# Zeroing the masked exponentials on GpSimd in place of a mask product on TensorE

## The chip, the cores and the metric

The kernel runs on one core of one Trainium2 chip. The metric is the device time of one launch in microseconds (us), lower is better; of the kernel before there are three runs. All engine names are those of the profile: PE is TensorE (PEld its weight loads), ACT ScalarE, DVE VectorE, POOL GpSimd, SP the engine that issues most DMAs.

## The reference, cut to what matters

32 sequences of 256 rows and 256 features attend to 77 context rows in 16 heads of 16, with a causal mask that lets row t see context rows 0 to t. A gated feed-forward with a shared part and a routed part of 8 experts follows.

```python
scores = jnp.einsum('bhqd,bhkd->bhqk', qh, kh) / jnp.sqrt(jnp.asarray(dh, q.dtype))
pad = mask[:, None, None, :]
causal = jnp.triu(jnp.ones((Sq, Sk), dtype=jnp.int32), k=1)[None, None]
merged = jnp.where(causal == 1, causal, pad)
scores = jnp.where(merged == 1, NEG_INF, scores)
attn = jax.nn.softmax(scores, axis=-1)
out = jnp.einsum('bhqk,bhkd->bhqd', attn, vh)
...
x = x + jnp.tanh(g_xattn[0]) * _L0_xattn_ref(_layernorm(x, axis=-1), ctx_1024, ctx_1024, L0_xattn_W, L0_xattn_b, mask_BxS2_if0)
x = x + jnp.tanh(g_ffn[0]) * _L0_ffn_ref(_layernorm(x, axis=-1), L0_ffn_w_in, L0_ffn_w_out, L0_ffn_w1, L0_ffn_w2, L0_ffn_wg, L0_ffn_we, L0_ffn_gb, L0_ffn_eb)
```

With 77 context rows the mask touches only the first 77 of the 256 query rows, a corner of 77 by 77 in every head.

## The kernel before

The kernel has two phases. Phase one runs attention, the shared feed-forward (`ffn`) and the routing for all sequences; phase two runs the experts tile by tile. The change lies in phase one.

**One list sets the order.** `phase_one` (L60) writes a list of stages `(name, b, k)`, and each engine walks through this same list and issues its own part of each stage, in order. So an engine that waits in one stage holds up all later stages on that engine. A pass i of the outer loop has 12 slots. Sequence b passes through them as a pipeline: its layer norm in pass b, its row maxima (`max`) in pass b+1, its scores, exponentials, values and the transposes `att` in pass b+2, its projection (`proj`), second norm and `x2T` in pass b+3. Below, "pass of sequence b" is the pass with the scores of b. After every second slot (1, 3, 5, 7, 9, 11) two pieces of the shared feed-forward are put into the list, 24 pieces for each pair of sequences. A piece below 16 is three matmuls of 512 columns (L712), a later one six of 256 (L729).

**Scores and values.** A step `scores` k handles four heads: four products of 256 columns (L620) into a pair of PSUM banks. Before them come two products of 154 columns (L615) that write the causal mask `cauT` (0 or -3e38) through the bf16 identity `identb` into the corners of the banks; the scores are added onto it. ACT turns the pair into exponentials `Pt` (L891), and each such step counts up the semaphore `P`. A step `values` k multiplies eight heads of `Pt` with `Vau` (L632) and waits for `P` of scores 2k+1, so for two exponentials.

**What GpSimd does.** In the order of the list: `bias` (L1449) adds the projection's bias to `x1`, once the DMA of `load_x1` (L500, issued by SP in slot 11 of the pass before) has landed; `keys` (L1424) spreads the keys, twice in each pass; `low` (L1375) makes the low part `gl` of the feed-forward's hidden values, at every pair of pieces with part 1, after ACT wrote the high part `gh` (L853), which ACT does behind the tanh (L932) of the same pair; `root` (L1382, L1384) takes the inverse square roots of the norms; `first` (L1442) adds the causal mask for the maxima; and in a routing round eight indirect DMAs scatter records (L1473), one at each piece of the list. Rounds (`ROUTES`, L43) come about every fourth pass.

**Places of the stages in a pass.** Before: scores in slots 1, 3, 5 and 7, values 0 in slot 5, values 1 in slot 8, `att` in slot 11. In slot 3 of each pass POOL has `keys` and a `low`; in the pass of an even sequence it also has a `low` in slot 7.

Of the kernel before, what the change touches and what calls it, by code (L numbers as in the profile page):

```python
# [7 lines left out]
BF = mybir.dt.bfloat16  # L8
I32 = mybir.dt.int32
ALU = mybir.AluOpType  # L10
# [3 lines left out]
P = 128  # L14
NB, S, D, K = 32, 256, 256, 77
# [6 lines left out]
NEG = -1e30  # L22
NEGP = -3e38
NEGB = -2.5e38
# [14 lines left out]
    "idb m8 ks0 va_zero va_one ones rec pre_zero pre wgh0 lb0 tgh brow pbias crow kcol ks1".split())}  # L39
GCON = {n: i + 7 for i, n in enumerate("ident caus cauT upb kint fold foldb".split())}  # L40

# [18 lines left out]
def phase_one():  # L60
# [31 lines left out]
    for i in range(NB + 3):  # L92
        slots = [[] for _ in range(12)]

        def put(b, stages):
            if 0 <= b < NB:
                for slot, name, k in stages:
                    slots[slot].append((name, b, k))

        if i % 2 == 1:  # L100
            put(i - 4, ((2, "logits", 0), (5, "logitsT", 0)))
            if i < NB + 1:
                put(i - 4, ((6, "store_x2", 0),))
        put(i - 2, ((1, "scores", 0), (3, "scores", 1), (5, "scores", 2), (5, "values", 0), (7, "scores", 3), (8, "values", 1),
                    (5 if i < 6 else 11, "load_x1", 0), (11, "att", 0)))
# [91 lines left out]
def build(nc, A, out):  # L197
    ctx = ExitStack()
    with ctx:
# [9 lines left out]

# [1 line left out]

# [3 lines left out]
        s = {n: ctx.enter_context(nc.semaphore("s_" + n)) for n in names.split()}  # L215
# [48 lines left out]
        sb = sbs(ctx)  # L264
        regr = sb("regr", [P, REG], R)
        ident = sb("ident", [P, P])
        Pt = sb("Pt", [P, H, S])
# [23 lines left out]
        sb = sbs(ph1)  # L291
# [12 lines left out]
        Xs = carve(KR, [2, 4, 2, S])  # L304
# [8 lines left out]
        identb = sb("identb", [P, P], BF)  # L313
        own8 = sb("own8", [P, 8])
        caus = sb("caus", [P, K], BF)
        cauT = sb("cauT", [K, K], BF)
        mhalf = sb("mhalf", [P, 2])
# [3 lines left out]
        fold = sb("fold", [20, 10])  # L321
# [5 lines left out]
        first = sb("first", [P, 2, K], BF)  # L327
# [4 lines left out]
        mr = sb("mr", [P, 2, 2])  # L332
# [11 lines left out]
        gl = sb("gl", [P, 4, 512], R)  # L344
        LGg = sb("LGg", [P, 16, 2])
        LGe = sb("LGe", [P, 16, 8])
        upb = sb("upb", [P, P], BF)
# [14 lines left out]
        kint = sb("kint", [P, 1], I32)  # L362
# [34 lines left out]
        ix = stage[:, 3232:3238].bitcast(I32).rearrange("p (j k) -> p j k", j=3)  # L397
# [5 lines left out]
        sb = sbs(ph2)  # L403
# [157 lines left out]
        def tensor(e):  # L561
            for stage_, b, k in order:
                h = b % 2
# [12 lines left out]
                elif stage_ == "max":  # L576
                    if k == 0:
                        e.wait_ge(s["xTh"], b + 1)
                    t, c = k // 2, k % 2
# [21 lines left out]
                elif stage_ == "scores":  # L601
                    if k == 0:
                        if b == 0:
                            e.wait_ge(s["ks1"], 1)
                            e.wait_ge(s["gcon"], GCON["cauT"])
                        if b == G:
                            e.wait_ge(s["ks1"], 2)
                        e.wait_ge(s[f"kd{ks}"], 96 * (b // G // 2 + 1))
                        e.wait_ge(s[f"xs{h}"], 48 * (b // 2 + 1))
                        e.wait_ge(s[f"mt{h}"], 16 * (b // 2 + 1))  # L610
# [3 lines left out]
                    for n in range(2):  # L614
                        e.matmul(pair[0:K, n, :].rearrange("k (j t) -> k j t", j=2)[:, :, 0:K], identb[0:K, 0:K],  # L615
                                 cauT[:, :].unsqueeze(1).broadcast_to([K, 2, K]), start=True, stop=False, skip_group_check=True)
                    for n in range(2):
                        p, bk = 2 * k + n, pair[:, n, :]
                        for j in range(2):
                            m = e.matmul(bk[0:K, j * S:(j + 1) * S], Kst[:, ks, j, p % 4, 2 * g + p // 4, :],  # L620
                                         Xs[:, h, p % 4, p // 4, :], start=False, stop=j == 1, skip_group_check=True)
                    m.then_inc(s["sc"], 1)
                elif stage_ == "values":
# [3 lines left out]
                    e.wait_ge(sem, v)  # L627
                    e.wait_ge(s["P"], 4 * b + 2 * k + 2)
                    for q in range(2):
# [22 lines left out]
                elif stage_ == "proj":  # L652
# [6 lines left out]
                    for t in range(2):  # L659
                        n = 0  # L660
# [698 lines left out]
        def gpsimd(e):  # L1359
# [17 lines left out]
            def root(n, b):  # L1377

                e.wait_ge(s[f"mom{n}"], 2 * b + 2)
                if b >= 1:  # L1380
# [6 lines left out]
            e.memset(caus[:, :], 0.0).then_inc(s["gcon"], 1)  # L1387
            e.memset(cauT[:, :], 0.0).then_inc(s["gcon"], 1)
            e.memset(upb[:, :], 1.0).then_inc(s["gcon"], 1)
            e.memset(mhalf[:, :], -0.5).then_inc(s["gcon"], 1)  # L1390
            e.memset(fold[:, :], 0.0).then_inc(s["gcon"], 1)
            e.wait_ge(s["gcon"], 6)
            e.affine_select(out=ident[:, :], in_=ident[:, :], compare_op=ALU.not_equal, fill=1.0, base=0,
                            pattern=[[-1, P]], channel_multiplier=1).then_inc(s["gcon"], 1)
            e.affine_select(out=caus[:, :], in_=caus[:, :], compare_op=ALU.is_ge, fill=NEG, base=0,
                            pattern=[[-1, K]], channel_multiplier=1).then_inc(s["gcon"], 1)
            e.affine_select(out=cauT[:, :], in_=cauT[:, :], compare_op=ALU.is_ge, fill=NEGP, base=0,
                            pattern=[[1, K]], channel_multiplier=-1).then_inc(s["gcon"], 1)
            e.affine_select(out=upb[:, :], in_=upb[:, :], compare_op=ALU.is_ge, fill=0.0, base=-1,
# [8 lines left out]
            for stage_, b, k in order:  # L1408
# [8 lines left out]
                elif stage_ == "keys":  # L1417
                    if k == 0:
# [3 lines left out]
                        if b >= 2:  # L1422
                            e.wait_ge(s["mm"], 4 * (b - 1))
                    e.tensor_tensor(Kbd[:, b % G, k, :, :], khi[:, b % G * 2 + k, :].bitcast(F).unsqueeze(1).broadcast_to([P, 8, K]),  # L1424
                                    own8[:, :].unsqueeze(2).broadcast_to([P, 8, K]), ALU.mult).then_inc(s["kbd"], 1)
                elif stage_ == "moments":
                    root(0, b)
# [127 lines left out]
```

## Time and profile before

| what | value |
|---|---|
| device time, median of three runs | 1164.55 us (1162.37 to 1165.7) |
| span of the profiled execution, first to last instruction | 1154.6 us |
| phase one in it | about 0 to 680 us |
| PE busy | 1105.4 us (96%) |
| DVE busy | 820.0 us (71%) |
| POOL busy | 519.1 us (45%) |
| ACT busy | 470.4 us (41%) |
| granted PE clock, mean over the span | 0.987 |

The device time of the profiled execution is not listed apart; its span is 9.95 us under the median of the runs, which lies around the instructions. Busy shares are means over stages with different limits. Because PE's matmuls overlap, its cost is read from the distance between starts, not from durations. In the timelines a row merges equal instructions that follow each other, with the first start, the length and the count; in square brackets stands the idle time of the engine before it and what ended that.

### The profile page before, as it was taken

How to read it: one execution, taken by the hardware profiler on the slowest of the kernel's cores; microseconds unless marked ns; L12 is line 12 of the kernel's file. 1: busy time of each engine (PE TensorE's matmuls, PEld its weight loads, DVE VectorE, ACT ScalarE, POOL GpSimd, SP SyncE). 2: the span in 40 equal slices, each digit the busy share in tenths (PEclk: the TensorE clock that was granted, in tenths of full speed). 3: DMA queues.
4: the chain of work that ended last, by engine and by line, in shares of the span. 5: the costliest groups of instructions: out<-in, count | busy, mean ns of one | idle time of the engine just before them, and what ended most of it. 6: DMA issues, size and time to landing. Idle time of an engine off the chain costs nothing.

```text
span 1154.6 us, 22482 instructions
## 1 busy us (share of the span) xinstructions
PE 1105.4 (96%) x7475; PEld 917.9 (80%) x7475; DVE 820.0 (71%) x1778; ACT 470.4 (41%) x722; POOL 519.1 (45%) x647
## 2 busy tenths in 40 slices
PE   5789999999999999999999899999999899999997
PEld 3557888787887788788788677788888788888886
DVE  7757686786786876876877576557544588888886
ACT  4565556545555555555654432223221111111111
POOL 5334447347356346456454523100000666666564
PEclk9989999999999999999999999999999899999999
DMA  8984647656665765764755311587662554555451
GB/s 158 242 191 80 145 98 128 132 118 107 136 125 93 148 131 115 123 141 102 118 117 109 70 46 38 199 263 236 209 211 93 162 160 150 164 162 157 147 177 65
DMA packets 106163, 160.65 MB, mean 139 GB/s; under 512 B 28828, under 2 KB 70718, under 8 KB 106048
## 3 DMA queue, kind: packets, MB, share of 16 engines
q1 hardware_dynamic: 94276, 121.18, 46.0%
q0 software_dynamic: 11776, 38.03, 10.6%
q8 instruction: 65, 1.06, 0.4%
q14 instruction: 46, 0.38, 0.1%
HBM read 75.24 MB, written 52.10 MB: 110 GB/s over the span
## 4 chain that ended last, share of the span: by engine, by line
PE 72%; DVE 10%; issue 8%; POOL 6%; ACT 2%; DMA 1%; POOLq 0%; ACTq 0%; DVEq 0%
PE ps L767 15%; PE ps L814 12%; PE ps L712 8%; PE ps L816 6%; PE ps L729 6%; PE ps L632 4%; PE ps L620 3%; PE ps L663 3%; PE ps L799 3%; POOL tab_dram L1473 2%; PE ps L586 2%; PE ps L590 2%; PE ps L615 1%; PE ps L697 1%; PE ps L686 1%
## 5 line engine op out<-in xcount | busy, mean ns | idle before, releaser
L814 PE MATMUL ps<-regr,gh 128*128 x600 | 221.5, 407 | 0.1
L891 ACT ACTIVATE Pt<-ps,pbias 77x1024 f32<-77x1024 f32 x128 | 141.4, 1105 | 107.4 <-PE ps L620 106.2
L816 PE MATMUL ps<-regr,gl 128*128 x600 | 170.0, 283 | 0.0
L814 PEld LDWEIGHTS ps<-regr,gh 128*128 128x128 f32 x600 | 113.8, 190 | 23.6 <-issue 0.5
L981 ACT ACTIVATE gh<-ps 128x512 fp32r<-128x512 f32 x75 | 44.8, 599 | 204.5 <-PE ps L799 204.5
L1192 DVE TENSOR_REDUCE mneg<-ps 128x8 f32<-128x616 f32 x128 | 100.5, 792 | 19.7 <-PE ps L590 19.6
L816 PEld LDWEIGHTS ps<-regr,gl 128*128 128x128 f32 x600 | 114.2, 190 | 0.0
L712 PE MATMUL ps<-x2h,winh 128*128 128x512 f32 x256 | 110.6, 432 | 0.5 <-DVE OHR L1096 0.5
L1375 POOL TENSOR_TENSOR gl<-gf,gh 128x512 fp32r<-128x512 f32 x64 | 82.5, 1290 | 50.4 <-ACT gh L853 50.1
L712 PE MATMUL ps<-x2h,winl 128*128 128x512 f32 x256 | 101.5, 396 | 0.0
L712 PE MATMUL ps<-x2l,winh 128*128 128x512 f32 x256 | 101.2, 395 | 0.0
L1449 POOL TENSOR_TENSOR x<-x,regf 128x512 f32<-128x512 f32 x32 | 41.1, 1284 | 130.4 <-DMA x<-in_x 130.4
L1361 POOL DMA_INDIRECT yt<-y_dram,Pt x73 | 75.5, 1035 | 53.2 <-PE ps L816 42.7
L1499 POOL DMA_INDIRECT out<-ot,Pt x75 | 77.6, 1035 | 41.3 <-issue 27.9
L1287 DVE SCALAR_TENSOR_TENSOR Pt<-Pt,ps 128x512 f32<-128x512 f32 x64 | 44.0, 688 | 69.0 <-ACT Pt L975 67.8
L975 ACT ACTIVATE Pt<-ps 128x512 f32<-128x512 f32 x64 | 38.3, 598 | 129.8 <-PE ps L767 129.8
L620 PE MATMUL ps<-regr 100*77 100x256 f32 x512 | 87.9, 295 | 0.0
L767 PE MATMUL ps<-regr,x2h 128*128 128x512 f32 x256 | 82.4, 396 | 0.0
L1424 POOL TENSOR_TENSOR regr<-regr,own 128x616 fp32r<-128x616 f32 x64 | 78.4, 1226 | 5.7 <-ACT regr L862 5.4
L1473 POOL DMA_INDIRECT tab_dram<-rec,slot x64 | 64.7, 1011 | 26.7 <-issue 13.3
L1320 DVE SCALAR_TENSOR_TENSOR ot<-ps,Pt,ot 128x256 f32<-128x256 f32 x150 | 72.6, 484 | 5.4
L632 PE MATMUL ps<-Pt,regf 77*32 77x256 f32 x1024 | 69.5, 389 | 6.1 <-ACT Pt L891 6.1
(201 smaller groups left out, 2681.7 us busy)
## 6 DMA issues: line engine op xcount, KB each, us to landing
regr<-regr SPq DMA_DIRECT2D x96, 256.0 KB, 5.9
y_dram<-Pt SPq DMA_DIRECT2D x64, 256.0 KB, 2.2
regf<-in_x SPq DMA_DIRECT2D x32, 256.0 KB, 2.9
x<-in_x SPq DMA_DIRECT2D x32, 256.0 KB, 7.2
y_dram<-res SPq DMA_DIRECT2D x32, 256.0 KB, 2.2
regr<-regr SPq DMA_DIRECT2D x96, 77.0 KB, 6.9
x_dram<-x2h SPq DMA_DIRECT2D x14, 512.0 KB, 3.0
x_dram<-x2l SPq DMA_DIRECT2D x14, 512.0 KB, 3.8
```

The costliest lines, as they stand in the source:

```text
L620: m = e.matmul(bk[0:K, j * S:(j + 1) * S], Kst[:, ks, j, p % 4, 2 * g + p // 4, :], Xs[:, h, p % 4, p // 4, :], start=False, stop=j == 1, ...
L632: m = e.matmul(bk[32 * j:32 * j + 32, q * S:(q + 1) * S], Vau[:, ks, g, n, :], Pt[0:K, n, :], start=True, stop=True)
L712: m = e.matmul(bk[:, :], w[:, cc, off:off + P], x[:, b % 2, cc, :], start=cc == 0 and n == 0, stop=cc == 1 and n == 2)
L767: i = e.matmul(bk[:, :], x[:, cc, k * P:(k + 1) * P], w[:, cc, half * 512:half * 512 + 512], start=n == 0, stop=n == 5)
L814: e.matmul(o, gh2[:, k % 3, fc, :], w2v[:, bass.ds(val, 1), fc, :, :].rearrange("p o h d -> p (o h) d"), start=fc == 0, stop=False, skip_g ...
L816: m = e.matmul(o[:, 0, :], gl2[:, k % 3, fc, :], w2v[:, bass.ds(val, 1), fc, 0, :].rearrange("p o d -> p (o d)"), start=False, stop=fc == ...
L891: e.activation(Pt[0:K, 4 * k:4 * k + 4, :].rearrange("k (n j) t -> k n (j t)", n=2), bank_of["sc", b, k][0:K, :, :], ACT.Exp, bias=pbias[: ...
L1192: e.tensor_reduce(mneg[:, h, t, :].rearrange("p (j q c) -> p c j q", j=2, c=2)[:, c], bank_of["mm", b, k][:, :, 0:4 * K].rearrange("p q (f ...
L1375: e.tensor_tensor(gl[:, fc, :], gf[:, n % 2, :], gh[:, fc, :].bitcast(F), ALU.subtract).then_inc(s["gl"], 1)
L1424: e.tensor_tensor(Kbd[:, b % G, k, :, :], khi[:, b % G * 2 + k, :].bitcast(F).unsqueeze(1).broadcast_to([P, 8, K]), own8[:, :].unsqueeze(2 ...
L1473: e.indirect_dma_start(tab, bass.IndirectOffsetOnAxis(ap=slot[:, j:j + 1], axis=0), rec[:, j, :], None, bounds_check=NC * NT - 1, oob_is_e ...
L1499: e.indirect_dma_start(out.rearrange("b s d -> (b s) d"), bass.IndirectOffsetOnAxis(ap=rt[:, k, 0:1].bitcast(I32), axis=0), ot[:, k % 8, : ...
```

## The change

The mask product L615 and its table `cauT` go. The scores now start the banks themselves (start=True). A new stage `causal` k, on GpSimd alone, waits for the exponentials of scores 2k+1 (`P`) and writes zero over the masked corner of eight heads in `Pt`, in place, 77 partitions by 8 by 77 elements, with one `affine_select`; it counts up the new semaphore `cz`. The step `values` k now waits for `cz` in place of `P`. In the list `causal` 0 stands in slot 4 and `causal` 1 in slot 8, values 0 moves from slot 5 to slot 6, and values 1 from slot 8 to slot 9.

```diff
-        put(i - 2, ((1, "scores", 0), (3, "scores", 1), (5, "scores", 2), (5, "values", 0), (7, "scores", 3), (8, "values", 1),
+        put(i - 2, ((1, "scores", 0), (3, "scores", 1), (4, "causal", 0), (5, "scores", 2), (6, "values", 0), (7, "scores", 3),
+                    (8, "causal", 1), (9, "values", 1),
                     (5 if i < 6 else 11, "load_x1", 0), (11, "att", 0)))
...
                     for n in range(2):
-                        e.matmul(pair[0:K, n, :].rearrange("k (j t) -> k j t", j=2)[:, :, 0:K], identb[0:K, 0:K],
-                                 cauT[:, :].unsqueeze(1).broadcast_to([K, 2, K]), start=True, stop=False, skip_group_check=True)
-                    for n in range(2):
                         p, bk = 2 * k + n, pair[:, n, :]
                         for j in range(2):
                             m = e.matmul(bk[0:K, j * S:(j + 1) * S], Kst[:, ks, j, p % 4, 2 * g + p // 4, :],
-                                         Xs[:, h, p % 4, p // 4, :], start=False, stop=j == 1, skip_group_check=True)
+                                         Xs[:, h, p % 4, p // 4, :], start=True, stop=True)
...
                     e.wait_ge(sem, v)
-                    e.wait_ge(s["P"], 4 * b + 2 * k + 2)
+                    e.wait_ge(s["cz"], 2 * b + k + 1)
...
+                elif stage_ == "causal":
+                    e.wait_ge(s["P"], 4 * b + 2 * k + 2)
+                    v = Pt[0:K, 8 * k:8 * k + 8, 0:K]
+                    e.affine_select(out=v, in_=v, compare_op=ALU.is_ge, fill=0.0, base=0,
+                                    pattern=[[0, 8], [1, K]], channel_multiplier=-1).then_inc(s["cz"], 1)
```

**On PE**, in the pass of an even sequence, around scores 2 (L620) and values 0 (L632). Before:

```order
L615 MATMUL ps<-cauT,identb 77x2x77 x2
L620 MATMUL ps<-regr 77x256 x4
L632 MATMUL ps<-Pt,regf 32x256 x8
L712 MATMUL ps<-x2h,winh 128x512
L712 MATMUL ps<-x2l,winh 128x512
L712 MATMUL ps<-x2h,winl 128x512
L712 MATMUL ps<-x2h,winh 128x512
L712 MATMUL ps<-x2l,winh 128x512
L712 MATMUL ps<-x2h,winl 128x512
L586 MATMUL ps<-regr 128x308 x2
```

The same place after (scores are L615 here, values L627, the feed-forward L707):

```order
L615 MATMUL ps<-regr 77x256 x4
L707 MATMUL ps<-x2h,winh 128x512
L707 MATMUL ps<-x2l,winh 128x512
L707 MATMUL ps<-x2h,winl 128x512
L707 MATMUL ps<-x2h,winh 128x512
L707 MATMUL ps<-x2l,winh 128x512
L707 MATMUL ps<-x2h,winl 128x512
L627 MATMUL ps<-Pt,regf 32x256 x8
L585 MATMUL ps<-regr 128x308 x2
```

The mask products are gone, and values 0 stands behind the pair of feed-forward pieces in place of ahead of it. Values 1 keeps its place, right behind such a pair, in these passes.

**On POOL**, in the pass of an even sequence, from the bias add on. Before:

```order
L1449 TENSOR_TENSOR x<-x,regf 128x512
L1424 TENSOR_TENSOR regr<-regr,own 128x616
L1375 TENSOR_TENSOR gl<-gf,gh 128x512
L1382 TENSOR_SCALAR ve<-mv 128x2
L1384 TENSOR_TENSOR rs<-ve,mhalf 128x2
L1442 TENSOR_TENSOR first<-pad,caus 128x77
L1375 TENSOR_TENSOR gl<-gf,gh 128x512
L1382 TENSOR_SCALAR ve<-mv 128x2
```

After:

```order
L1446 TENSOR_TENSOR x<-x,regf 128x512
L1416 TENSOR_TENSOR regr<-regr,own 128x616
L1370 TENSOR_TENSOR gl<-gf,gh 128x512
L1421 AFFINE_SELECT Pt<-Pt 77x8x77
L1377 TENSOR_SCALAR ve<-mv 128x2
L1379 TENSOR_TENSOR rs<-ve,mhalf 128x2
L1439 TENSOR_TENSOR first<-pad,caus 128x77
L1370 TENSOR_TENSOR gl<-gf,gh 128x512
L1421 AFFINE_SELECT Pt<-Pt 77x8x77
L1377 TENSOR_SCALAR ve<-mv 128x2
```

Causal 0 comes behind the bias add, the second `keys` and a `low`; causal 1 comes behind the next `low`.

**On POOL in the pass of an even sequence with a routing round**, after:

```order
L1446 TENSOR_TENSOR x<-x,regf 128x512
L1416 TENSOR_TENSOR regr<-regr,own 128x616
L1470 DMA tab_dram<-rec,slot 110592x4
L1370 TENSOR_TENSOR gl<-gf,gh 128x512
L1470 DMA tab_dram<-rec,slot 110592x4
L1421 AFFINE_SELECT Pt<-Pt 77x8x77
```

Two scatters more stand between the bias add and causal 0. The orders of DVE and SP are unchanged, and ACT's differs only in four copies of the values' output in the first and last passes.

## Rows read from the trace of the kernel before

**Rows 1.** Head of the page, and shares of the chain that ended last.

```profile
span 1154.6 us, 22482 instructions
...
PE 72%; DVE 10%; issue 8%; POOL 6%; ACT 2%; DMA 1%; POOLq 0%; ACTq 0%; DVEq 0%
```

**Rows 2.** Busy times by stretch: window, PE, PEld, DVE, ACT, POOL, clock, DMA share, GB/s.

```profile
300.00:400.00 100.00, 98.34 (x770) 79.99 (x769) 76.50 (x180) 56.38 (x85) 50.73 (x66) 1.00 0.64 121
```

**Rows 3.** Timeline of PE in pass 19: start, length, engine, line, operation, tiles, shapes, count.

```profile
407.87 0.30 PE L615 MATMUL ps<-cauT,identb 77*77 77x154 bf16 x2
407.96 0.67 PE L620 MATMUL ps<-regr 100*77 100x256 f32 x4
408.48 0.28 PE L729 MATMUL ps<-woh,gh 128*128 128x256 f32 x1
408.60 0.28 PE L729 MATMUL ps<-wol,gh 128*128 128x256 f32 x1
```

**Rows 4.** Groups of instructions by line and shape, POOL: count, busy us, mean ns, idle.

```profile
L1424 POOL TENSOR_TENSOR regr<-regr,own 128x616 fp32r<-128x616 f32 x64 | 78.4, 1226 | 5.7 <-ACT regr L862 5.4 <-issue 0.2
...
L1416 POOL COPY regf<-regf 77x512 f32<-77x512 f32 x16 | 9.7, 606 | 0.0
...
L1406 POOL TENSOR_SCALAR_AFFINE_SELECT fold<-fold 20x10 f32<-20x10 f32 x2 | 0.4, 184 | 0.1
L1393 POOL TENSOR_SCALAR_AFFINE_SELECT ident<-ident 128x128 f32<-128x128 f32 x1 | 0.3, 288 | 0.2 <-POOL fold L1391 0.2
```

**Rows 5.** Timeline of ACT and PE in pass 19, scores 3 and values 1.

```profile
418.05 1.11 ACT L891 ACTIVATE Pt<-ps,pbias 77x1024 f32<-77x1024 f32 x1
...
419.38 1.07 PE L632 MATMUL ps<-Pt,regf 77*32 77x256 f32 x16
```

**Rows 6.** Timeline of POOL in pass 18.

```profile
390.53 1.28 POOL L1449 TENSOR_TENSOR x<-x,regf 128x512 f32<-128x512 f32 x1 [7.78 <-DMA x<-in_x]
...
392.95 1.28 POOL L1375 TENSOR_TENSOR gl<-gf,gh 128x512 fp32r<-128x512 f32 x1
394.32 0.22 POOL L1382 TENSOR_SCALAR ve<-mv 128x2 f32<-128x2 f32 x1
...
398.23 1.30 POOL L1375 TENSOR_TENSOR gl<-gf,gh 128x512 fp32r<-128x512 f32 x1 [2.61 <-ACT gh L853]
```

**Rows 7.** Timeline of SP, the load that pass 18's bias add waits for.

```profile
383.23 0.60 SPq L500 DMA_DIRECT2D x<-in_x  x1
```

**Rows 8.** Timeline of PE in pass 18.

```profile
391.33 1.07 PE L632 MATMUL ps<-Pt,regf 77*32 77x256 f32 x16
392.34 0.50 PE L712 MATMUL ps<-x2h,winh 128*128 128x512 f32 x1
...
393.82 0.45 PE L586 MATMUL ps<-regr 128*128 128x308 f32 x2
...
396.93 1.07 PE L632 MATMUL ps<-Pt,regf 77*32 77x256 f32 x16
```

**Rows 9.** Timeline of ACT in pass 18, slot 7.

```profile
397.04 0.60 ACT L932 ACTIVATE tt<-ps 128x512 f32<-128x512 f32 x1 [0.28 <-PE ps L712]
397.53 0.62 ACT L853 ACTIVATE gh<-gf 128x512 fp32r<-128x512 f32 x1
```

**Rows 10.** Timeline of POOL in pass 20, with a routing round.

```profile
432.86 1.28 POOL L1449 TENSOR_TENSOR x<-x,regf 128x512 f32<-128x512 f32 x1 [2.08 <-DMA x<-in_x]
...
437.97 0.99 POOL L1473 DMA_INDIRECT tab_dram<-rec,slot  x1 [0.17 <-issue]
```

**Rows 11.** Timeline of PE in pass 20, the end of the pair in slot 5.

```profile
435.49 0.44 PE L586 MATMUL ps<-regr 128*128 128x308 f32 x2
```

**Rows 12.** Waits between 650 and 654 us: who for whom, us, times, longest.

```profile
PE ps L673 <- DVE xn L1230: 2.6, 1, 2.6
```

**Rows 13.** Busy times by stretch around that wait, columns as in Rows 2.

```profile
651.00:654.00 3.00, 0.73 (x7) 0.77 (x8) 1.58 (x4) 0.07 (x1) 2.40 (x5) 1.00 0.72 92
654.00:657.50 3.50, 3.50 (x14) 2.95 (x12) 2.24 (x5) 0.53 (x1) 2.10 (x2) 0.51 0.04 7
```

More of the change, by code:

```diff
@@ L22 @@
 NEG = -1e30
-NEGP = -3e38
 NEGB = -2.5e38
@@ L39 @@
     "idb m8 ks0 va_zero va_one ones rec pre_zero pre wgh0 lb0 tgh brow pbias crow kcol ks1".split())}
-GCON = {n: i + 7 for i, n in enumerate("ident caus cauT upb kint fold foldb".split())}
+GCON = {n: i + 6 for i, n in enumerate("ident caus upb kint fold foldb".split())}
 ROUTES = [(4 * c - 4, 8, c) for c in range(1, NCH - 2, 2)] + [(4 * c, 4, c) for c in (NCH - 2, NCH - 1)]
@@ L315, in build @@
         caus = sb("caus", [P, K], BF)
-        cauT = sb("cauT", [K, K], BF)
         mhalf = sb("mhalf", [P, 2])
@@ L604, in tensor @@
                             e.wait_ge(s["ks1"], 1)
-                            e.wait_ge(s["gcon"], GCON["cauT"])
                         if b == G:
@@ L1387, in gpsimd @@
             e.memset(caus[:, :], 0.0).then_inc(s["gcon"], 1)
-            e.memset(cauT[:, :], 0.0).then_inc(s["gcon"], 1)
             e.memset(upb[:, :], 1.0).then_inc(s["gcon"], 1)
@@ L1391, in gpsimd @@
             e.memset(fold[:, :], 0.0).then_inc(s["gcon"], 1)
-            e.wait_ge(s["gcon"], 6)
+            e.wait_ge(s["gcon"], 5)
             e.affine_select(out=ident[:, :], in_=ident[:, :], compare_op=ALU.not_equal, fill=1.0, base=0,
@@ L1396, in gpsimd @@
                             pattern=[[-1, K]], channel_multiplier=1).then_inc(s["gcon"], 1)
-            e.affine_select(out=cauT[:, :], in_=cauT[:, :], compare_op=ALU.is_ge, fill=NEGP, base=0,
-                            pattern=[[1, K]], channel_multiplier=-1).then_inc(s["gcon"], 1)
             e.affine_select(out=upb[:, :], in_=upb[:, :], compare_op=ALU.is_ge, fill=0.0, base=-1,
```

2 rows, old and new, of the table names are left out of this document.

## The prediction

> **What bounds the kernel now.** I read the head of the page and the chain that ended last: most of the span is PE's own work [rows 1]. Then the busy times by stretch: in the steady part of phase one PE is busy 98.3 of 100 us at the full clock, POOL half of the time [rows 2]. So phase one runs at PE's pace, and two things count: how many us PE no longer issues, and how long PE stands still at values, which from now on wait for an engine that is half idle on average but takes its work in a fixed order. The average says nothing on the second; for that I read the timelines of PE, ACT, POOL and SP over single passes, and ask at each values step: when does PE get there, and when could POOL have finished the zeroing in its new place. Passes are named by their sequence; 28 passes (4 to 31) run beside the feed-forward, 14 even and 14 odd.
>
> **What the change takes from PE.** From the first mask product to the first matmul behind the scores pass 408.48 - 407.87 = 0.61 us, in which four scores products of 256 columns are issued. Two products of 256 columns start 0.12 us apart in the same listing, so the four take 0.48, and the two mask products 0.13 us [rows 3]. Of these pairs there are 4 x 32 = 128: 16.6 us of PE's time less. Nothing hides it in the steady part. The table `cauT` is made once, ahead of everything here, and is charged at nothing.
>
> **Price of one zeroing.** The trace has no affine_select of 8 x 77 = 616 elements. It has two of f32, 10 and 128 elements in a row, at 184 and 288 ns: 0.88 ns for each further element, so 184 + 606 x 0.88 = 717 ns. A copy of 512 elements took 606 ns; an operation with two inputs of 616 elements took 1226 ns [rows 4]. Bounds are 0.6 and 1.23 us, and I take 0.72, because affine_select and the copy read one tile, as these do. The Trainium skill (GPSIMD Engine Reference, section 4.1 Engine selection) calls GpSimd about line-rate for one input and some 2x slower than VectorE for two, which speaks for the lower end. By its figure for one input (section 3.1, 1.03 cycles an element at 1.2 GHz) my estimate would be 0.53 us and the sum about 8 us lower; the rows here that I have do not reach that size, so it stays at 0.72.
>
> **The chain of one values step.** From the end of an exponential to the values it releases lie 419.38 - 419.16 = 0.22 us [rows 5], and from ACT's end of `gh` (397.53 + 0.62 = 398.15) to POOL's start 0.08 us [rows 6, 9]. I use these two as the latencies into PE and into POOL.
>
> **Odd passes, values 1.** The values already start right at the exponential's end [rows 5]. POOL is idle there. New start: 419.16 + 0.08 + 0.72 + 0.22 = 420.18 against 419.38, a wait of 0.80 us. 14 times: 11.2 us. Values 0 of odd passes have room, since the move behind the pair gives PE 1.5 us of other work (393.82 - 392.34, as in the even pass [rows 8]). This is what the move is paid for, and here it is enough.
>
> **Even passes, values 1.** Here POOL has to make `gl` of the pair in slot 7 before causal 1. ACT's tanh waits for this very pair, then comes `gh`, then POOL's `gl` ends at 398.23 + 1.30 = 399.53 [rows 6, 9]. PE goes from this pair straight to values 1, at 396.93 [rows 8]. With the zeroing and the latency: 399.53 + 0.72 + 0.22 = 400.47, a wait of 3.54 us. It is a chain that starts at PE's own pair, so a later PE doesn't shorten it. 14 times: 49.6 us. Behind POOL's zeroing are queued the `root` for the next norm, which PE's next steps (two pieces, `x2T` in slot 10) don't wait for in this pass: no further cost.
>
> **Even passes, values 0.** POOL sits 7.78 us idle until the load for the bias add has landed. SP issued it at 383.23, it is 7.3 us under way, and then bias, keys and `gl` run without a gap to 392.95 + 1.28 = 394.23 [rows 6, 7]. Zeroing and latency: 395.17. PE in the new order would get to values 0 when the pair in slot 5 is through: 393.82 less the 1.01 us that values 0 took ahead of it (392.34 - 391.33), less three mask products of this pass, 0.39: 392.42 [rows 8]. A wait of 2.75 us. The load is issued behind steps of the pass before that follow PE, so this doesn't shrink in the steady state. 6 passes (6, 10, ... 26): 16.5 us.
>
> **Even passes with a routing round, values 0.** Two scatters more stand ahead of causal 0; the last ends at 437.97 + 0.99 = 438.96, so values could start at 439.90. PE gets there at 435.49 - 1.01 - 0.39 = 434.09 [rows 8, 10, 11]. A wait of 5.8 us, in 7 passes (8, 12, ... 28 and 30): 40.6 us.
>
> **The first four passes** are bound by chains, not by PE; of their eight values steps I charge half with 0.80: 3 us. In pass 30 a wait of 2.6 us at `x2T`, for a norm that POOL delays [rows 12], is already there and goes under the new one: 2.6 less.
>
> **The clock.** After the 2.6 us in which PE stood at L673 the granted clock fell from 1.00 (2.4 GHz) to 0.51 (1.2 GHz) for 3.5 us, while PE was busy all the time [rows 12, 13]: 3.5 x 0.49 = 1.7 us lost. The new waits over 3 us are 14 + 7 = 21; if each is followed by such a fall, they cost 21 x 1.7 = 36 us. I charge these, and none for the six waits of 2.75 us. The Trainium skill (TensorE: Matmul & The Clock Gate, section Why this matters for your kernels) advises against idle gaps between bursts of matmuls because they bring the array to its lower clock; by that rule the sum is 1302 us or more, without it 1266. It speaks against this change.
>
> **Sum.** Against the span: 1154.6 - 16.6 + 11.2 + 49.6 + 16.5 + 40.6 + 3 - 2.6 + 36 = 1292.3 (the waits alone 118.3). The 9.95 us between the span and the median of the runs stay: 1302 us.
>
> **Rivals.**
> - *The waits without the clock.* If the fall behind L673 had another reason than the wait, or most of the new waits bring none, the sum is 1302 - 36 = 1266, with a spread of 1250 to 1282. For it: one row on the clock is thin. Against it: the waits are longer than that one. Chance 0.20.
> - *A slow zeroing.* If the pattern of eight rows costs what a two-input operation costs, 1.23 us, each of the 41 waits (14 + 14 + 6 + 7) grows by 0.51: 21 us, 1323. Chance 0.12, 1316 to 1345.
> - *POOL comes early to causal 0.* If the load or the scatters run ahead of a PE that is held up, the first waits go (57 us, and 7 x 1.7 = 12 of the clock): about 1233, or 1195 to 1242. For it: scatters and loads are not all tied to PE. Against it: SP's queue and the routing steps are in the same list as PE's pieces. Chance 0.12.
> - *Faster.* The zeroing is hidden behind the pair of pieces that now stands ahead of values, at both places and in every pass. Then only the mask products count: 1164.55 - 16.6 = 1148. It decides at 16.6 / 28 = 0.6 us of waiting in a pass; the odd passes alone already have 0.8 and the even ones over 6. For it: POOL is only half busy. Chance 0.04; that it comes to rest within 0.3% 0.03.
>
> **How the numbers follow.** The forecast, 1302, has 0.49 with a spread of 1282 to 1316. The range should hold 8 in 10: it takes in this case, the one without the clock, and nearly all of the slow zeroing, and leaves out most of the early POOL and the faster case: 1245 to 1340. A difference of 0.3% (3.5 us) is about what a measurement of this kernel can tell from no change. Slower by over that: 0.49 + 0.20 + 0.12 + 0.12 = 0.93; within it 0.03; faster 0.04.
>
> **What would show the steps.** In the profile after: no product of 154 columns; 64 zeroings of about 0.72 us; PE waiting for POOL at values for 110 to 125 us in all, in an even pass some 3.5 us at values 1 and 2.75 or 5.8 us at values 0, in an odd pass 0.8 us at values 1 only; POOL's wait for the load as long as before; the clock at 0.5 for a few us behind the long waits; phase two unchanged. I am wrong if `gl` of slot 7 doesn't follow PE's pair, if POOL reaches causal 0 before PE reaches values 0, or if the clock stays up.

## The result: 1320.24 us, 13.5% slower

The changed kernel takes 1320.24 us (median of 6 runs, 1317.9 to 1325.57), the kernel before 1164.04 (6 runs, 1162.37 to 1165.7): a ratio of 1.1347, 95% interval 1.1321 to 1.1372. The forecast was 1302 us, with a range of 1245 to 1340.

The head of the page after, with its PE clock by slices and the chain that ended last; it answers to [rows 1].

```profile
span 1316.2 us, 22030 instructions
...
PEclk8799988988989979799898897999999989999999
...
PE 58%; issue 18%; POOL 16%; DVE 4%; DMA 2%; ACT 1%; SPq 0%; POOLq 0%; ACTq 0%; DVEq 0%
```

POOL has grown from 6% to 16% of the chain, and the clock has dips all through the first 25 slices. Busy times by stretch of both kernels (window, PE, PEld, DVE, ACT, POOL, clock, DMA share, GB/s), phase one and the rest; first before, then after:

```profile
0.00:680.00 680.00, 644.06 (x4988) 523.01 (x4989) 498.97 (x1187) 369.48 (x556) 339.88 (x470) 0.98 0.63 125
680.00:1154.00 474.00, 461.36 (x2489) 394.93 (x2487) 320.99 (x593) 100.90 (x166) 179.27 (x177) 0.99 0.49 159
```

```profile
0.00:841.00 841.00, 682.71 (x4732) 545.31 (x4733) 504.25 (x1187) 370.11 (x556) 388.83 (x532) 0.89 0.51 101
841.00:1316.00 475.00, 461.59 (x2489) 394.88 (x2487) 320.85 (x592) 100.95 (x166) 179.47 (x177) 0.99 0.50 159
```

All of it lies in phase one: 161 us more, against 1 us in the rest. There PE is idle for 841 - 683 = 158 us, before for 680 - 644 = 36: 122 us more. The other 39 us are PE's own work made slower by a mean clock of 0.89 in place of 0.98, less what the mask products took. DVE's busy time for the same 1187 instructions is 504 us against 499, so the zeroing on POOL does not slow DVE to speak of.

Who PE waits for after (us in total, times, longest), and the group of the zeroings (min/median/max ns):

```profile
PE ps L627 <- POOL Pt L1421: 131.3, 48, 8.0
...
PE ps L585 <- DVE mneg L1187: 5.5, 10, 1.4
```

```profile
L1421 POOL TENSOR_SCALAR_AFFINE_SELECT Pt<-Pt x64: 764/777/1136, 31.3 to 831.1; 77x616 f32<-77x616 f32 x64
```

**Pass 18 after**, the one that [rows 6] and [rows 8] show before. POOL:

```profile
469.98 1.28 POOL L1446 TENSOR_TENSOR x<-x,regf 128x512 f32<-128x512 f32 x1 [7.81 <-DMA x<-in_x]
471.21 1.22 POOL L1416 TENSOR_TENSOR regr<-regr,own 128x616 fp32r<-128x616 f32 x1
472.39 1.26 POOL L1370 TENSOR_TENSOR gl<-gf,gh 128x512 fp32r<-128x512 f32 x1
473.60 0.77 POOL L1421 TENSOR_SCALAR_AFFINE_SELECT Pt<-Pt 77x616 f32<-77x616 f32 x1
...
483.00 1.26 POOL L1370 TENSOR_TENSOR gl<-gf,gh 128x512 fp32r<-128x512 f32 x1 [7.24 <-ACT gh L848]
484.21 0.80 POOL L1421 TENSOR_SCALAR_AFFINE_SELECT Pt<-Pt 77x616 f32<-77x616 f32 x1
```

PE at values 0 and values 1 of the same pass, and then at values 1 of the odd pass 19:

```profile
474.52 1.93 PE L627 MATMUL ps<-Pt,regf 77*32 77x256 f32 x16 [2.61 <-POOL Pt L1421]
...
485.16 1.94 PE L627 MATMUL ps<-Pt,regf 77*32 77x256 f32 x16 [3.39 <-POOL Pt L1421]
```

```profile
510.36 1.07 PE L627 MATMUL ps<-Pt,regf 77*32 77x256 f32 x16 [0.73 <-POOL Pt L1421]
```

The load still keeps POOL idle for 7.8 us in this pass, as before; then bias, keys, gl and zeroing run on end, and PE waits 2.61 us. At values 1 it waits 3.39 us behind a gl that waited for ACT, which waited for PE. The odd pass has 0.73 us. In the first four passes, seven of the eight values steps wait too, 12.7 us in all; the longest is values 1 of pass 0:

```profile
39.21 1.93 PE L627 MATMUL ps<-Pt,regf 77*32 77x256 f32 x16 [3.11 <-POOL Pt L1421]
```

The stretches around the two waits of pass 18:

```profile
472.00:474.50 2.50, 0.00 (x0) 0.01 (x1) 2.39 (x8) 0.00 (x0) 2.42 (x4) 0.99 0.79 205
474.50:481.30 6.80, 6.78 (x33) 4.89 (x34) 2.63 (x7) 2.31 (x3) 1.18 (x3) 0.50 0.01 4
481.30:484.70 3.40, 0.47 (x2) 0.04 (x1) 2.26 (x4) 1.12 (x2) 1.70 (x2) 1.00 0.01 2
484.70:491.50 6.80, 6.34 (x32) 4.41 (x33) 1.56 (x7) 1.31 (x3) 1.67 (x5) 0.50 0.25 48
```

PE stands still for 2.5 us and then works for 6.8 us at 0.50 (1.2 GHz); it stands again, in part at the full clock, and works 6.8 us at 0.50 once more. The same values step took 1.07 us before [rows 8] and 1.93 here.

In pass 20, with a routing round, POOL up to the zeroing, and PE at values 0; it answers to [rows 10] and [rows 11]:

```profile
523.75 1.28 POOL L1446 TENSOR_TENSOR x<-x,regf 128x512 f32<-128x512 f32 x1 [2.52 <-DMA x<-in_x]
...
528.84 1.00 POOL L1470 DMA_INDIRECT tab_dram<-rec,slot  x1 [0.17 <-issue]
529.82 0.82 POOL L1421 TENSOR_SCALAR_AFFINE_SELECT Pt<-Pt 77x616 f32<-77x616 f32 x1
```

```profile
530.78 1.93 PE L627 MATMUL ps<-Pt,regf 77*32 77x256 f32 x16 [5.72 <-POOL Pt L1421]
```

With two scatters more between the bias add and the zeroing, the wait is 5.72 us here.

### The profile page after: what moved, and what is told of

Its sections match the earlier page's. It is cut to its first block, busy times and chain, and to the rows that moved or that the text cites. A ratio compares the mean times of both kernels' runs of the same rounds, so it can differ in the third digit from the quotient of the medians.

```text
span 1316.2 us, 22030 instructions
## 1 busy us (share of the span) xinstructions
PE 1144.3 (87%) x7219; PEld 940.2 (71%) x7219; DVE 825.1 (63%) x1778; ACT 471.1 (36%) x722; POOL 568.3 (43%) x709
## 3 DMA queue, kind: packets, MB, share of 16 engines
q8 instruction: 63, 1.03, 0.4%
## 4 chain that ended last, share of the span: by engine, by line
PE 58%; issue 18%; POOL 16%; DVE 4%; DMA 2%; ACT 1%; SPq 0%; POOLq 0%; ACTq 0%; DVEq 0%
PE ps L762 14%; PE ps L809 11%; PE ps L707 7%; PE ps L811 5%; PE ps L627 4%; POOL tab_dram L1470 4%; PE ps L724 3%; POOL Pt L1421 3%; POOL gl L1370 3%; POOL regr L1416 3%; PE ps L794 3%; PE ps L636 2%; PE ps L658 2%; POOL rs L1379 1%; PE ps L668 1%
## 5 line engine op out<-in xcount | busy, mean ns | idle before, releaser
L627 PE MATMUL ps<-Pt,regf 77*32 77x256 f32 x1024 | 86.9, 466 | 131.3 <-POOL Pt L1421 131.3
L627 PEld LDWEIGHTS ps<-Pt,regf 77*32 77x32 f32 x1024 | 34.5, 124 | 162.9 <-issue 154.9
L707 PE MATMUL ps<-x2h,winh 128*128 128x512 f32 x256 | 115.9, 453 | 0.9 <-DVE OHR L1091 0.9
L893 ACT ACTIVATE regf<-ps 128x512 f32<-128x512 f32 x64 | 38.3, 598 | 195.4 <-PE ps L627 195.2
L707 PE MATMUL ps<-x2h,winl 128*128 128x512 f32 x256 | 107.1, 418 | 0.0
L707 PE MATMUL ps<-x2l,winh 128*128 128x512 f32 x256 | 106.9, 418 | 0.0
L615 PE MATMUL ps<-regr 100*77 100x256 f32 x512 | 97.7, 316 | 1.5 <-DMA regr<-regr 1.5
L1251 DVE TENSOR_TENSOR gf<-tt,ps 128x512 f32<-128x512 f32 x64 | 43.1, 673 | 72.8 <-issue 62.2
L1421 POOL TENSOR_SCALAR_AFFINE_SELECT Pt<-Pt 77x616 f32<-77x616 f32 x64 | 50.8, 794 | 73.6 <-ACT Pt L886 73.6
```

The lines of the kernel that those rows point to most:

```text
L627: m = e.matmul(bk[32 * j:32 * j + 32, q * S:(q + 1) * S], Vau[:, ks, g, n, :], Pt[0:K, n, :], start=True, stop=True)
L707: m = e.matmul(bk[:, :], w[:, cc, off:off + P], x[:, b % 2, cc, :], start=cc == 0 and n == 0, stop=cc == 1 and n == 2)
L1421: e.affine_select(out=v, in_=v, compare_op=ALU.is_ge, fill=0.0, base=0, pattern=[[0, 8], [1, K]], channel_multiplier=-1).then_inc(s["cz"], 1)
```

## The experiments

Theory: the loss is PE's standing at values, set by what POOL's list has ahead of each zeroing (the bias add with its late load, gl, scatters), and paid a second time through the clock. Rivals: the zeroing itself or the hand-over is the price, wherever it stands; the clock matters little; the move of the values steps costs. All ratios are against runs of the kernel before on the same chip; its median there was 1159.4 to 1164.5 us. Differences between two ratios are turned into us with 1164. Twelve kernels were run.

### The mask product alone: e1 and e2

e1 is the kernel before without the mask products and with nothing in their place:

```diff
-                        e.matmul(pair[0:K, n, :].rearrange("k (j t) -> k j t", j=2)[:, :, 0:K], identb[0:K, 0:K],
-                                 cauT[:, :].unsqueeze(1).broadcast_to([K, 2, K]), start=True, stop=False, skip_group_check=True)
...
-                                         Xs[:, h, p % 4, p // 4, :], start=False, stop=j == 1, skip_group_check=True)
+                                         Xs[:, h, p % 4, p // 4, :], start=True, stop=True)
```

> The kernel before without the 256 mask products of the scores, and with nothing in their place: the causal mask is left out of the attention. It measures the saving alone. Theory: phase one runs at PE's pace, so 128 pairs at 0.13 us come off the time: 1164 - 16.6 = 1147 us, ratio 0.986. Rival: PE's products ran under waits for other engines (ACT's exponentials, DVE's maxima), and less than a third of it shows: 1158 to 1164 us.

Measured: 1153.27 us, ratio 0.9945 (0.9911 to 0.9978): 6.4 us saved, between 2.6 and 10.3, not 16.6. That is a little over a third of the products' price, nearer to the rival's "less than a third" than to the theory. Whom PE waits for between 100 and 620 us, first before, then in e1:

```profile
PE ps L615 <- DVE regf L1212: 2.9, 10, 0.3
PE ps L586 <- DVE mneg L1192: 1.6, 6, 0.3
PE ps L673 <- DVE xn L1230: 0.7, 2, 0.5
```

```profile
PE ps L617 <- DVE regf L1209: 4.3, 12, 0.9
PE ps L586 <- DVE mneg L1189: 3.0, 7, 0.7
PE ps L670 <- DVE xn L1227: 2.7, 5, 0.6
PE ps L598 <- DVE regr L994: 1.0, 5, 0.4
PE ps L574 <- DVE x L1218: 0.9, 3, 0.4
```

With less on PE, the steps whose data DVE makes come too early: these waits grow from 5.2 to 11.9 us in the stretch, so in these 25 passes DVE takes back 6.7 of the 13 us (25 x 4 x 0.13) that the products cost. e2 is the opposite edit: the changed kernel with the mask products put back.

```diff
+                    for n in range(2):
+                        e.matmul(pair[0:K, n, :].rearrange("k (j t) -> k j t", j=2)[:, :, 0:K], identb[0:K, 0:K],
+                                 cauT[:, :].unsqueeze(1).broadcast_to([K, 2, K]), start=True, stop=False, skip_group_check=True)
...
-                                         Xs[:, h, p % 4, p // 4, :], start=True, stop=True)
+                                         Xs[:, h, p % 4, p // 4, :], start=False, stop=j == 1, skip_group_check=True)
```

> The changed kernel with the mask products of the scores put back (the corner is masked twice). It measures what the mask costs where PE now waits anyway. Theory: of the 128 pairs, the three ahead of each wait at values 0 (13 even passes, 39 pairs) are swallowed by the wait; the other 89 cost 0.13 us each in full, because DVE, which took most of the saving in e1, now has slack: 11.6 us more, ratio to the kernel before 1.145 where the changed one has 1.135. Rival: DVE still takes two thirds, as in e1: 4 us more, ratio 1.138.

Measured: 1328.52 us, ratio 1.1408 (1.1386 to 1.143), against 1.1347 of the changed kernel: 0.0061 x 1164 = 7 us more. This lies between the two numbers, and the intervals of the two ratios, taken at their ends, leave 1.6 to 12.7 us; e2 doesn't decide. PE waits a little less for POOL than the 131.3 us of the changed kernel, as the theory has it:

```profile
PE ps L633 <- POOL Pt L1430: 127.9, 46, 7.8
```

So the mask was worth 6.4 us in the kernel before; what it was worth in the changed kernel is known only within those bounds.

### The clock: e6

e6 is the changed kernel with PE's waits in the even passes filled by matmuls that nothing reads:

```diff
+                    if b >= 4 and b % 2 == 0:
+                        for _ in range(13 if k else 24 if b % 4 == 0 and b > 4 or b == 30 else 10):
+                            e.matmul(bk[:, :], winh[:, 0, 0:P], winh[:, 0, 0:512], start=True, stop=True)
                     e.wait_ge(s["cz"], 2 * b + k + 1)
```

> The changed kernel; in even passes from 4 on PE issues products of 512 columns into the bank that the values will overwrite, ahead of its wait for the zeroing: 10 at values 0 (24 in routing passes) and 13 at values 1, at 0.23 us each a little less than the wait they stand in. They compute nothing that is used. Theory: the waits cost twice, once as such (some 122 us more idle time than before) and once through the clock, which is at half speed for 184 us in phase one after, against 20 us before; the products keep the clock up and the time falls by 50 to 65 us, to 1255 to 1270 us, with a mean clock near 0.98. Rival: the low clock lies under the waits and costs little: 1310 to 1325 us, or more where the products overrun the waits.

Measured: 1266.51 us, ratio 1.0915 (1.0824 to 1.1005), so 0.0432 x 1164 = 50 us less than the changed kernel, with more work on PE. The page's PE clock by slices, and what is left of PE's waits for POOL:

```profile
PEclk9999999999999999999999999999999999999999
```

```profile
PE ps L630 <- POOL Pt L1424: 37.6, 48, 3.1
```

The zeroings are as before (median 775 ns against 777); only the waits were filled with matmuls. So the low clock behind the waits costs some 50 us, and the waits without it leave 1.0915. A few of the products may also have overrun a wait, so 50 is if anything low.

### POOL's order: e3, e4 and e5

e3, causal 1 ahead of gl:

```diff
-                    (8, "causal", 1), (9, "values", 1),
+                    (7, "causal", 1), (9, "values", 1),
```

> The changed kernel with one edit: causal 1 stands in slot 7 right behind scores 3, so ahead of POOL's gl of the pair in that slot. Theory: the 3.4 us waits at values 1 of even passes come from that gl; they fall to about 0.9 us where POOL has no scatters (7 passes), and stay at some 2 to 3 us in the 7 routing passes, where two scatters of the pair in slot 5 are ahead. Waits 7 x 2.5 + 7 x 1 = 25 us less, and the low clock behind them some 15 us less: 1270 to 1285 us. Rival: POOL's place among its other work doesn't matter and the waits are the price of the hand-over and the zeroing (0.78 us) itself: 1315 to 1325 us.

Measured: 1258.12 us, ratio 1.0839 (1.0766 to 1.0912). One edit of a slot number gives back 0.0508 x 1164 = 59 us of 157. POOL and PE in an even pass without a round:

```profile
438.84 0.77 POOL L1421 TENSOR_SCALAR_AFFINE_SELECT Pt<-Pt 77x616 f32<-77x616 f32 x1
...
445.11 0.77 POOL L1421 TENSOR_SCALAR_AFFINE_SELECT Pt<-Pt 77x616 f32<-77x616 f32 x1 [4.11 <-ACT Pt L886]
446.69 1.29 POOL L1370 TENSOR_TENSOR gl<-gf,gh 128x512 fp32r<-128x512 f32 x1 [0.80 <-ACT gh L848]
```

```profile
439.76 1.07 PE L627 MATMUL ps<-Pt,regf 77*32 77x256 f32 x16 [2.54 <-POOL Pt L1421]
446.03 1.07 PE L627 MATMUL ps<-Pt,regf 77*32 77x256 f32 x16 [0.58 <-POOL Pt L1421]
```

The wait at values 1 is 0.58 us where it was 3.39, that at values 0 is as before. It went further than expected: in the routing passes too no wait over 0.92 us stands at values 1. That POOL catches up on the scatters of slot 5 while PE stands at values 0 fits this, and e5 bears it out: there PE no longer stands at values 0, and values 1 of these passes waits 6.2 us.

e4, causal 0 ahead of the bias add, and so also of the keys and the gl of slot 3:

```diff
-        put(i - 2, ((1, "scores", 0), (3, "scores", 1), (4, "causal", 0), (5, "scores", 2), (6, "values", 0), (7, "scores", 3),
+        put(i - 2, ((1, "scores", 0), (3, "scores", 1), (3, "causal", 0), (5, "scores", 2), (6, "values", 0), (7, "scores", 3),
...
-        put(i - 3, ((2, "bias", 0), (1, "attT", 0), (4, "proj", 0), (7, "norm2", 0), (10, "x2T", 0)) if i < NB + 2 else
+        put(i - 3, ((3, "bias", 0), (1, "attT", 0), (4, "proj", 0), (7, "norm2", 0), (10, "x2T", 0)) if i < NB + 2 else
```

> The changed kernel with causal 0 in slot 3 right behind scores 1, and the bias add moved from slot 2 to slot 3 behind it. So POOL zeroes before it waits for the load. Theory: the waits at values 0 of even passes (2.6 and 5.7 us, 58 us in all) go to nearly nothing, and the falls of the clock behind them (some 30 us) with them: 1225 to 1245 us. Rival: the late load and the scatters only shift the wait to the projection (DVE needs the bias add) and from there to PE: less than half of it comes back, over 1275 us.

Measured: 1278.27 us, ratio 1.1025 (1.0944 to 1.1106): 37 us back, less than half, so the total came out at the rival's number, by another way than the rival named. PE at values 0 and 1 of pass 20, and PE's waits:

```profile
505.86 1.07 PE L627 MATMUL ps<-Pt,regf 77*32 77x256 f32 x16
517.65 1.94 PE L627 MATMUL ps<-Pt,regf 77*32 77x256 f32 x16 [7.44 <-POOL Pt L1421]
```

```profile
PE ps L627 <- POOL Pt L1421: 101.1, 36, 9.3
PE ps L724 <- POOL gl L1370: 9.1, 13, 0.7
```

The wait at values 0 is gone, as the theory has it; the load, the keys and gl, which all stood ahead of causal 0, were not tried apart. But in the routing pass the one at values 1 has grown to 7.44 us: PE is no longer held at values 0 while POOL works off its scatters, so POOL's backlog meets PE at the next zeroing. And in 13 odd passes PE now waits 0.7 us for a gl that stands behind the zeroing and the bias add.

e5 is both edits together.

> The edits of e3 and e4 together: causal 0 behind scores 1 in slot 3 with the bias add behind it, causal 1 behind scores 3 in slot 7. Theory: outside the routing passes neither the load, nor gl stands ahead of a zeroing, so each pass keeps the 0.8 us of the hand-over at values 1; in the 7 routing passes the scatters of slots 3 and 5 and the late bias add still stand ahead of causal 1: 7.4 us in e4, less the gl (1.3), so some 5 to 6 us. Waits 21 x 0.8 + 7 x 5.5 = 55 us, low clock 7 x 3 = 21 us, the mask's saving 6 to 16 us: 1164 + 60 to 70 = 1220 to 1235 us, ratio 1.05 to 1.06. Rival: something not yet seen (port or semaphore cost of the zeroing on every pass) keeps it near e3: over 1.075.

Measured: 1249.65 us, ratio 1.0752 (1.0723 to 1.078), above the theory's 1.06 and on the rival's border. PE's waits for POOL at values:

```profile
PE ps L627 <- POOL Pt L1421: 73.7, 36, 8.0
```

From pass 4 on nothing but one 0.28 us is left at values 0. At values 1 each pass outside the routing rounds keeps 0.5 to 0.8 us (1.5 in the last), as the theory has it; the seven routing passes wait 6.2 us in six cases and 8.0 in pass 30. The theory had 55 us of waits. It left out the first four passes, 12 of the 74 us, and the 9 us that PE waits for gl, as in e4; that is most of its miss. No cost of the zeroing in every pass beyond the 0.8 us is seen, as the rival would have it.

### What stands ahead in the routing passes: e8, e9 and e11

e8 is e5 with the last four scatters of a round behind causal 1:

```diff
+                    if j >= 4 and at_ < last:
+                        held.append(j)
+                    elif j >= 0:
+                        scatter(j)
...
+                    while k and held:
+                        scatter(held.pop(0))
```

> e5 with the last four of a round's eight scatters moved behind causal 1 of the pass (POOL alone; the same eight are made). Theory: POOL's order is all that is left in the routing passes, so their waits fall from over 5 us to about 1 us; 28 x 0.85 = 24 us of waits stay and no fall of the clock in the steady part: ratio 1.005 to 1.02, clock 0.98. Rival: in the routing passes POOL lacks time, not order (8 scatters, 2 keys, 2 or 3 gl, the roots in one pass); the four scatters then hold up the roots of the next norm or the next causal 0, and the wait moves there: ratio 1.03 or more.

Measured: 1204.67 us, ratio 1.0355 (1.0328 to 1.0383): 0.0397 x 1164 = 46 us back against e5, by POOL's order alone. A routing pass of e8, POOL's zeroing and PE at values 1 and at the scores of the next pass:

```profile
382.38 0.77 POOL L1426 TENSOR_SCALAR_AFFINE_SELECT Pt<-Pt 77x616 f32<-77x616 f32 x1
383.34 1.10 POOL L1373 DMA_INDIRECT tab_dram<-rec,slot  x1 [0.18 <-issue]
```

```profile
383.30 1.07 PE L627 MATMUL ps<-Pt,regf 77*32 77x256 f32 x16 [1.28 <-POOL Pt L1426]
...
390.75 0.67 PE L615 MATMUL ps<-regr 100*77 100x256 f32 x4 [1.40 <-DVE regf L1207]
```

The wait of 6.2 us is 1.28. In pass 30 2.9 us stay. Both are right in part: the order was the cause, but a new wait of up to 1.4 us for DVE stands at the next pass's scores in seven places, and the ratio is over 1.03 as the rival had it.

e9 moves scores 3 and causal 1 to slot 6, e11 also keeps the mask product for sequences 0 to 4 and moves the second keys step to slot 4:

```diff
-        put(i - 2, ((1, "scores", 0), (3, "scores", 1), (3, "causal", 0), (5, "scores", 2), (6, "values", 0), (7, "scores", 3),
-                    (7, "causal", 1), (9, "values", 1),
+        put(i - 2, ((1, "scores", 0), (3, "scores", 1), (3, "causal", 0), (5, "scores", 2), (6, "values", 0), (6, "scores", 3),
+                    (6, "causal", 1), (9, "values", 1),
```

and, in e11 alone, with `CUT = 5`:

```diff
-        put(i, ((1, "keys", 0), (3, "keys", 1)))
+        put(i, ((1, "keys", 0), (3 if i < 7 else 4, "keys", 1)))
...
-                    for n in range(2):
+                    for n in range(2 if b < CUT else 0):
```

> e8 with scores 3 and causal 1 in slot 6, so that the product for the maxima (0.57 us on PE) also lies between scores 3 and values 1. Theory: it covers most of the 0.8 us of the hand-over, 0.25 us stay in each of 28 passes (7 us), against the 6 us that e1 showed as the saving of the mask: ratio 0.995 to 1.005. Rival: the hand-over costs more than its own time because the row maxima of slot 6 come later and DVE, which e1 showed to be next in line, is hit: ratio over 1.01.

> e9 with two edits: sequences 0 to 4 keep the mask product and the wait for the exponentials (no zeroing), and the second keys step of a pass goes to slot 4, behind the gl of slot 3. Theory: what e9 still has over the kernel before is the first passes (each step of values some 0.9 us, about 8 us), PE's waits for gl in odd passes (9 us at 13 places), and the low clock there; both go: ratio 1.00 to 1.01. Rival: the clock's falls in e9 (ten, against four before) come from a steady loss in every pass, and stay: ratio 1.015 or more.

Measured: e9 1189.09 us, ratio 1.0218 (1.0192 to 1.0244), so its theory's number is missed; e11 1165.99 us, ratio 1.0028 (1.0009 to 1.0047), as expected. PE's waits in e9 and in e11:

```profile
PE ps L627 <- POOL Pt L1426: 18.5, 17, 3.0
PE ps L615 <- DVE regf L1207: 10.2, 12, 1.4
PE ps L724 <- POOL gl L1370: 9.2, 13, 0.7
```

```profile
PE ps L634 <- POOL Pt L1436: 13.4, 14, 3.3
PE ps L622 <- DVE regf L1214: 8.8, 7, 1.4
```

In e9 the hand-over at values 1 is covered, as the theory has it. What the theory left out is the clock, which stood at half speed for 68 us of phase one in e9 (mean over the span 0.965) against 20 us in the kernel before. The rival's number holds, its reason isn't shown: e8 already had 8.3 us of the waits of scores for DVE.

So with the zeroing placed for POOL's order, and the mask product kept in the first passes, all but 0.3% of the loss is gone. It doesn't beat the kernel before. The rows fit that DVE and what is left of the hand-over take what a pass saves on PE, but this was not tried apart; e12 below, with scores 3 and the values in the same slots and no zeroing, is at 1.0011.

### The zeroing's own time: e7

e7 is the changed kernel with each zeroing made twice:

```diff
+                    for n in range(2):
+                        if n:
+                            e.wait_ge(s["cy"], 2 * b + k + 1)
...
+                                        pattern=[[0, 8], [1, K]], channel_multiplier=-1).then_inc(s["cz" if n else "cy"], 1)
```

> The changed kernel with each zeroing made twice, one behind the other. Theory: POOL's time counts where PE waits for it: at 14 values 1 of even passes, 13 values 0 of even passes and 14 values 1 of odd passes, 41 x 0.85 = 35 us, and some us in the first four passes, and more low clock where a 1.6 us wait now stands in odd passes: 1355 to 1375 us. Rival: waits are set by the load and gl alone and POOL has room for a second zeroing: under 1335 us.

Measured: 1374.06 us in one run, 54 us more. PE's waits for POOL grow from 131.3 to 174.7 us:

```profile
PE ps L627 <- POOL Pt L1424: 174.7, 48, 8.7
```

43 us of it are waits, near the 35 that were expected plus the first passes. In pass 18 values 1 waits 4.22 us in place of 3.39, in pass 19 1.57 in place of 0.73: each second zeroing makes the wait 0.83 to 0.84 us longer, a little more than the 0.777 us of its own duration. The rest fits the clock, whose mean over the span fell from 0.927 to 0.904.

### The move of the values steps: e10 and e12

e10 is the kernel before with the values steps in their new slots:

```diff
-        put(i - 2, ((1, "scores", 0), (3, "scores", 1), (5, "scores", 2), (5, "values", 0), (7, "scores", 3), (8, "values", 1),
+        put(i - 2, ((1, "scores", 0), (3, "scores", 1), (5, "scores", 2), (6, "values", 0), (7, "scores", 3), (9, "values", 1),
```

> The kernel before with one part of the change alone: values 0 in slot 6 and values 1 in slot 9; mask product and the wait for the exponentials as before, nothing on GpSimd. Theory: the move costs nothing by itself, since values 0 feeds only the transposes of slot 11: ratio 0.998 to 1.002. Rival: the later release of the exponentials' tile and of the PSUM bank holds up ACT's next exponentials or the banks: ratio over 1.005.

Measured: 1157.24 us, ratio 0.9949 (0.9931 to 0.9967). It computes the same and is 0.5% faster than the kernel before (6 runs, on one chip), which neither side had foreseen. So the move is no part of the loss. e12 adds the earlier scores 3 of e9:

```diff
-        put(i - 2, ((1, "scores", 0), (3, "scores", 1), (5, "scores", 2), (6, "values", 0), (7, "scores", 3), (9, "values", 1),
+        put(i - 2, ((1, "scores", 0), (3, "scores", 1), (5, "scores", 2), (6, "values", 0), (6, "scores", 3), (9, "values", 1),
```

> e10 (values 0 in slot 6, values 1 in slot 9, mask product as before, no zeroing) and scores 3 in slot 6 too, ahead of the product for the maxima. Theory: in the kernel before PE stands some 0.2 us at values 1 of each pass for the second exponential; with the product for the maxima in between that goes, on top of the gain of e10: 28 x 0.2 = 5 us, ratio 0.990. Rival: e9 showed that scores 3 in slot 6 brings its own waits at the scores of the next pass, and the gain of e10 is partly the spread between runs: ratio 0.995 to 1.000.

Measured: 1162.33 us, ratio 1.0011 (0.9987 to 1.0035): no difference. Where the 6 us of e10 come from, and whether they would show again on another chip, stays open. PE's waits for DVE between 100 and 620 us are 4.0 us in e10 against 5.2 before, which is too little to name a cause.

## Why the prediction was right

By its own steps:

- **The waits** where PE bounds were forecast almost exactly: for the 41 steps from pass 4 on 117.9 us, measured 118.6. By groups: values 1 of even passes 49.6 forecast, 47.3 measured (3.39 us in pass 18 against 3.54); values 0 of even passes without a round 16.5 and 16.1 (2.61 against 2.75); with a round 40.6 and 44.2 (5.72 in pass 20 against 5.8, but 8.0 in pass 30); odd passes 11.2 and 11.0. e3 and e8 show gl and the scatters as causes by moving them alone; e4 shows the same for what stands ahead of causal 0 as a whole, and that the load leads it is read from the timeline.
- **The first four passes** were under-charged: 3 us for half of eight steps, 12.7 measured in seven. So PE waited 131.3 us for POOL at values, over the 110 to 125 that the prediction named as its sign. PE's idle time in phase one grew by less, 122 us, because 6 us of waits at values for ACT's exponentials and 3 us of waits for a norm, the one of [rows 12] among them, were no longer there.
- **That the waits don't shrink** as PE falls back: POOL's wait for the load is 7.81 us after, 7.78 before, in pass 18, and much the same in the other even passes without a round.
- **The zeroing**: 0.72 us forecast, 0.777 measured.
- **The clock** was the right mechanism with too small a term: 36 us were charged, e6 shows some 50. PE's work in phase one was at half speed in 30 stretches and for 184 us, PE busy in 150 of them, against 4 stretches and 20 us before. Of the 21 waits over 3 us that were charged, 19 were followed by a fall, or had it begin in their last us or two. The step "none for the six waits of 2.75 us" failed: all six, 2.57 to 3.10 us long, were followed by one too. So did the length of a fall, taken from a single one of 3.5 us: more than half of the 30 lasted 6.8 us or longer. No row supported the bound at 3 us. The Trainium skill's advice against idle gaps between bursts of matmuls (TensorE: Matmul & The Clock Gate, section Why this matters for your kernels) holds here, with the 50 us of e6.
- **The mask product**: for the kernel before, the step "nothing hides it in the steady part" failed, 6.4 us in e1 where 16.6 were charged. PE's 98% busy did not say that DVE was right behind. For the changed kernel the step isn't shown wrong: there PE stands at values, which leaves DVE time, and the prediction's net is 16.6 less the 0.39 us by which PE comes earlier to each of 13 waits, 11.5 us, within the 1.6 to 12.7 of e2.
- **The sum** was 23.9 us too low against the profile (1292.3 and 1316.2). PE's idle time grew by 122 us where 118.3 were charged, its busy time by 39 where 36 - 16.6 = 19.4 were, and phase two by 1. So 19 of the 24 us lie in PE's busy time. If the mask products took their 16.6 us from it, the low clock took 39 + 16.6 = 55, near the 50 of e6.
- **From the span to the median** 9.95 us were added, where after it is 1320.24 - 1316.2 = 4.0. In every run listed with its span the time is 1.7 to 1.8 us over the span; the rest of the 9.95 is that the profiled execution of the kernel before was shorter than all six of its runs. So this term hid 6 us of the sum's miss, and 18 are left in the median.
- **Of the rivals**: 1320.24 lies 4 us over the spread of the forecast's own case (1282 to 1316) and in the band of the slow zeroing (1316 to 1345), but not for its reason, since the zeroing took 0.777 us and not 1.23. The waits without the clock (1266) are refuted by e6 and by the granted clock in pass 18. "POOL comes early to causal 0" did not happen, and "faster" would have needed under 0.6 us of waiting a pass, where the odd passes alone had 0.73.

## What to carry to other kernels

An engine that is half idle can still be late at every hand-over when its work comes in a fixed order: look at what it has to do, and to wait for, just ahead of the new step, not at its busy share. A step that a bound engine waits for belongs directly behind the event that releases it, ahead of everything that waits for a transfer; moving one stage by one slot gave 59 us here. The zeroing can be had for nearly nothing this way (e11, ratio 1.0028), but not at a gain. And PE's waits of 2.6 to 8 us cost twice in this kernel, once as such and, in nearly every case, once as a low clock behind it.

## What the runs showed of the hardware

- Filling PE's waits with matmuls whose results nobody reads made the kernel 50 us faster (e6, mean clock 0.99 against 0.927), although PE had more to do.
- After a wait of 2.61 us (pass 18) the granted clock was at 0.50 for 6.8 us of almost unbroken matmuls, twice as long as the fall that [rows 13] show of the kernel before. It was so for two of the six waits at values 0 without a round; the other four were followed by 3.4 us at half speed, as in pass 6, where the wait of 2.60 us ended at 158.8 (columns as in [rows 2]):

```profile
160.42:163.84 3.42, 3.42 (x14) 3.07 (x13) 2.64 (x7) 1.80 (x3) 0.00 (x0) 0.50 0.00 0
```

- An affine_select of 77 x 616 f32 elements on GpSimd took 777 ns (764 to 1136), between the copy of 512 elements (606 ns) and the two-input operation of 616 (1226 ns) of [rows 4]. Its figure from the Trainium skill, the 0.53 us estimated from the GPSIMD Engine Reference (section 3.1), was too low; the measurement decides.
